# An attention row split anew: seven tiles scaled on ScalarE, outputs scaled with their maximum on VectorE

## The reference, cut to what matters

```python
attn = jnp.einsum('bhnd,bhmd->bhnm', q, k) * attn_scale
attn, a_scale = fq_act(attn)
x_int = x / sf                       # log_int_softmax
x_int = x_int - x_int.max(axis=-1, keepdims=True)
exp_int, _ = _int_exp(x_int, sf)
exp_sum = exp_int.sum(axis=-1, keepdims=True)
ratio = exp_sum / exp_int            # rounded, then to the nearest power of two
attn = jnp.where(mask, 0.0, 2.0 ** (-qlog))
out = jnp.einsum('bhnm,bhmd->bhnd', attn, v)
out, _ = fq_act(out)                 # needs max and min of all outputs
```

## Time and profile before

| quantity | value |
|---|---|
| median of three runs | 1063.03 us (1061.05 to 1063.34) |
| the profiled execution | 1064.02 us, span 1062.2 us |
| VectorE busy | 880.3 us, 83% of the span |
| TensorE busy | 740.5 us, 70% |
| ScalarE busy | 711.8 us, 67% |
| GpSimd busy | 170.0 us, 16% |
| mean granted TensorE clock | 0.837 |

### The profile page before, as it was taken

One profiled execution on the slowest core, in us unless ns is written; L12 is line 12 of the kernel. 1 busy time (PEld: TensorE's weight loads), 2 busy tenths in 40 slices (PEclk: granted clock), 3 DMA queues, 4 the chain that ended last, 5 costly groups with the idle time before them and its releaser, 6 DMA issues. The chain is left out here.

```text
span 1062.2 us, 23653 instructions
## 1 busy us (share of the span) xinstructions
PE 740.5 (70%) x6503; PEld 515.3 (49%) x6504; DVE 880.3 (83%) x2386; ACT 711.8 (67%) x1376; POOL 170.0 (16%) x274
## 2 busy tenths in 40 slices
PE   3772396748888367667667666766532895999997
PEld 3552144425555234434334344433322784889896
DVE  5888986888888799999999999999969632666776
ACT  0353464947888699989989889899750563445543
POOL 5841400016554000000000000000007320000000
PEclk9995598978999687887887788788657676999999
DMA  7000000001111111111110111110040003455452
GB/s 250 3 2 0 0 1 1 0 4 39 37 37 35 32 31 24 25 25 23 23 23 23 26 25 25 23 24 19 12 156 12 1 2 110 147 184 196 166 203 87
DMA packets 84369, 54.61 MB, mean 51 GB/s; under 512 B 53832, under 2 KB 83304, under 8 KB 84072
## 3 DMA queue, kind: packets, MB, share of 16 engines
q1 hardware_dynamic: 83304, 53.97, 16.7%
q0 software_dynamic: 1024, 0.13, 0.2%
HBM read 11.77 MB, written 3.76 MB: 15 GB/s over the span
## 5 line engine op out<-in xcount | busy, mean ns | idle before, releaser
L1370 DVE SCALAR_TENSOR_TENSOR expo<-expo,con,pow 128x153 f32<-128x153 f32 x480 | 146.1, 377 | 1.1 <-ACT expo L1279 1.1
L1148 PE MATMUL at_rem<-word,ident_half 128*128 128x459 f16 x160 | 64.4, 402 | 101.1 <-ACT expo L1279 99.6
L1279 ACT ACTIVATE expo<-at_rem,con 128x459 f32<-128x459 f32 x160 | 95.5, 641 | 12.8 <-PE at_rem L1149 11.4
L953 DVE TENSOR_REDUCE rs_ends<-rs_banks 128x770 f32 (+1 forms) x96 | 91.4, 959 | 14.7 <-PE rs_banks L924 13.7
L873 ACT ACTIVATE rs_banks<-rs_banks 128x770 f32<-128x770 f32 x96 | 76.4, 798 | 25.4 <-PE rs_banks L916 24.2
L1408 DVE CUSTOM_DVE_ANT_0 weight_top<-weight_top,line 128x2448 uint16<-128x2448 uint16 x64 | 86.7, 1354 | 7.1 <-ACT line L1271 3.5
L1148 PEld LDWEIGHTS at_rem<-word,ident_half 128*128 128x128 f16 x160 | 15.6, 97 | 151.7 <-ACT expo L1279 145.6
L1236 ACT ACTIVATE word<-at_banks 128x459 uint8<-128x459 f32 x160 | 79.5, 562 | 8.7 <-PE at_banks L779 8.6
L1229 ACT ACTIVATE pT_all<-at_pT 128x768 bf16<-128x768 int16 (+3 forms) x160 | 79.1, 566 | 7.6 <-PE at_pT L1171 5.7
L774 PE MATMUL at_banks<-pick,row_top 128*128 128x459 bf16 x160 | 72.3, 452 | 13.7 <-ACT word L1236 7.4
L1271 ACT ACTIVATE line<-weight_top 128x1224 f32<-128x1224 f32 x64 | 74.1, 1159 | 10.3 <-DVE weight_top L1398 10.2
(11 more groups left out here) (393 smaller groups left out, 2134.7 us busy)
## 6 DMA issues: line engine op xcount, KB each, us to landing
qk<-vt SPq DMA_DIRECT2D x64, 384.0 KB, 3.0
rs_kb<-qk SPq DMA_DIRECT2D x128, 28.7 KB, 1.9
kb<-qk SPq DMA_DIRECT2D x128, 28.7 KB, 1.9
patches<-in_patches SPq DMA_DIRECT2D x4, 768.0 KB
vi<-vt SPq DMA_DIRECT2D x32, 96.0 KB, 2.0
out<-vi SPq DMA_DIRECT2D x32, 96.0 KB, 1.8
pj_w<-in_w SPq DMA_DIRECT2D x1, 2304.0 KB, 8.3
qb<-qk SPq DMA_DIRECT2D x128, 6.0 KB, 1.8
```

What stands on the lines that cost most here:

```text
L953: v.tensor_reduce(ends[:, :, n, 5 * b:5 * b + 5], banks[:, slot(u, b), :, 0:5 * W].rearrange("p i (t n) -> p i t n", n=W), AX, ALU.max).th ...
L1148: pe.matmul(out, identh[:, :], bank(word, b).bitcast(F16), start=True, stop=False)
L1279: act.activation(bank(ex, b), rem[:, (u + b) % 2, 0:3 * N], ACT.Square, scale=2.0 ** 24, bias=c(5)).then_inc(sq_done, 1)
L1370: ins = v.scalar_tensor_tensor(ex[:, t, :], ex[:, t, :], c(7), pw[:, t, :].bitcast(BF16), ALU.add, ALU.mult, accum_out=tot[:, t:t + 1])
```

## The change

- `both_shares` (ScalarE) multiplies tiles 8 to 14, not 12 to 14. VectorE multiplies tiles 0 to 7 only. `line_of` 1 waits for ScalarE's own products alone.
- `collect` (ScalarE) is gone. VectorE reads the outputs from PSUM, scales, stores and takes their maximum in one TENSOR_TENSOR_REDUCE (`extreme(pair, 0)`), before its pass over `pT_all`; the minimum is taken in the other step of a pair, as before.
- `corner` (ScalarE) and its buffer `p_image` are gone. TensorE transposes those columns straight from the weights, with twelve transposes of 32 columns in the place of three of 128. VectorE's product therefore waits for all of `turn` of the sample before.
- VectorE's order within a step is changed: reciprocal ahead of `octave`, product ahead of `pow`. Its stage is written out for all 34 steps; the other engines keep their loop.

```diff
-                            src = high[:, t, 0:NT] if t < RT else pi[:, 4 * (t - RT):4 * (t - RT) + 4, :].rearrange("p j n -> p (j n)")
-                            mm = pe.transpose(pT[:, slot, j * P:(j + 1) * P], src, identb[:, :])
+                            if t < RT:
+                                mm = pe.transpose(pT[:, slot, j * P:(j + 1) * P], high[:, t, 0:NT], identb[:, :])
+                            else:
+                                for q in range(4):
+                                    mm = pe.transpose(pT[32 * q:32 * q + 32, slot, j * P:(j + 1) * P], high[:, 4 * (t - RT) + q, IW:N], identb[:, :])
...
-                    act.activation(pi[:, :, :].bitcast(I16), high[:, 0:H, IW:N].bitcast(I16), ACT.Copy).then_inc(pi_done, 1)
...
-                    for t in range(H, RT):
+                    for t in range(HALF, RT):
                         ins = act.activation(top[:, t, :], ex[:, t, :], ACT.Copy, scale=inv[:, t:t + 1])
...
-                    act.activation(out_f32(m)[:, pair, :], po[:, 0:HT * N], ACT.Copy, scale=P_UNIT).then_inc(out_done, 1)
...
+                    if kk == 0:
+                        v.wait_ge(pv_done, pair * 2 + 2)
+                        v.tensor_tensor_reduce(out, po[:, 0:HT * N], c(2).to_broadcast([P, HT * N]), 1.0, -BIG, ALU.mult, ALU.max, accum_out=at).then_inc(out_done, 1)
...
-                        for h, half in enumerate(halves):
...
-                            v.tensor_tensor(top[:, heads, :], ex[:, heads, :], share, ALU.mult).then_inc(w_done, 1)
+                        heads = halves[0]
+                        share = inv[:, heads].unsqueeze(2).to_broadcast([P, HALF, N])
+                        v.tensor_tensor(top[:, heads, :], ex[:, heads, :], share, ALU.mult).then_inc(w_done, 1)
...
-                steps(v, body)
+                for n in range(B + 2):
+                    body(n // 2, n % 2)
```

More of the change, by code:

```diff
@@ L1041, in attention @@
         ends_done = k.sem("at_ends_done")
-        pi_done, pj_done, tr_done, ev_done, pv_done, out_done = sem(
-            "pi_done", "pj_done", "tr_done", "ev_done", "pv_done", "out_done")
+        pj_done, tr_done, ev_done, pv_done, out_done = sem(
+            "pj_done", "tr_done", "ev_done", "pv_done", "out_done")
         pj_loaded, a_done = k.sem("pj_loaded"), k.sem("at_a_done")
@@ L1266, in line_of @@
                 def line_of(n, h):
-                    act.wait_ge(w_done, n * 2 + h + 1)
-                    if h == 1:
+                    if h == 0:
+                        act.wait_ge(w_done, n + 1)
+                    else:
                         act.wait_ge(a_done, n + 1)
@@ L1274, in squares @@
                     if not first(n, 1):
-                        act.wait_ge(w_done, n * 2 - (1 if which[0] == 0 else 0))
+                        act.wait_ge(w_done, n)
                     for b in which:
@@ L1279, in squares @@
                         act.activation(bank(ex, b), rem[:, (u + b) % 2, 0:3 * N], ACT.Square, scale=2.0 ** 24, bias=c(5)).then_inc(sq_done, 1)
-                def collect(n, pair):
-                    act.wait_ge(pv_done, n + 1)
-                    act.activation(out_f32(m)[:, pair, :], po[:, 0:HT * N], ACT.Copy, scale=P_UNIT).then_inc(out_done, 1)
                 def body(i, kk):
-                    now, mid, last, gone = (batch(i, kk, lag) for lag in range(4))
+                    now, mid, last = (batch(i, kk, lag) for lag in range(3))
                     if now is not None:
                         distances(now[0])
-                    if gone is not None and gone[1] == 1:
-                        collect(gone[0], gone[2])
                     for chunk in chunks_at(i, kk):
@@ L1294, in body @@
                     if last is not None:
-                        corner(last[0])
                         ranks(last[0], last[1])
@@ L1310, in _ @@
                 steps(act, body)
-                collect(B - 1, B // 2 - 1)
             @block.vector
@@ L1347, in extreme @@
                 def extreme(pair, kk):
[L1349 to L1354 removed]
+                    out, at = out_f32(m)[:, pair, :], m["pj_ext"][:, kk, pair:pair + 1]
+                    if kk == 0:
+                        v.wait_ge(pv_done, pair * 2 + 2)
+                        v.tensor_tensor_reduce(out, po[:, 0:HT * N], c(2).to_broadcast([P, HT * N]), 1.0, -BIG, ALU.mult, ALU.max, accum_out=at).then_inc(out_done, 1)
+                    else:
                         v.wait_ge(out_done, pair + 1)
[L1356 removed]
+                        v.tensor_reduce(at, out, AX, ALU.min, negate=True).then_inc(ends_done, 1)
                 def body(i, kk):
@@ L1375, in body @@
                         v.tensor_scalar(tot[:, :], tot[:, :], LOWER, SHARE, ALU.max, ALU.mult).then_inc(tot_done, 1)
+                        v.wait_ge(tot_done, nb + 1)
+                        v.reciprocal(inv[:, :], tot[:, :]).then_inc(inv_done, 1)
                     if yf is not None:
@@ L1382, in body @@
                     if yb is not None:
-                        v.wait_ge(tot_done, nb + 1)
-                        v.reciprocal(inv[:, :], tot[:, :]).then_inc(inv_done, 1)
+                        v.wait_ge(inv_done, nb + 1)
+                        if not first(nb, 1):
+                            v.wait_ge(tr_done, nb * GROUPS)
+                        heads = halves[0]
+                        share = inv[:, heads].unsqueeze(2).to_broadcast([P, HALF, N])
+                        v.tensor_tensor(top[:, heads, :], ex[:, heads, :], share, ALU.mult).then_inc(w_done, 1)
                     if yf is not None:
@@ L1387, in body @@
                         v.tensor_scalar(pw[:, :, :], oct_[:, :, :], -128.0, 128.0 * (2048 + 63), ALU.mult, ALU.add).then_inc(pw_done, 1)
[L1388 to L1391, removed]
-                        for h, half in enumerate(halves):
[L1393 to L1397, removed]
-                            v.tensor_tensor(top[:, heads, :], ex[:, heads, :], share, ALU.mult).then_inc(w_done, 1)
+                    if kk == 0 and pair is not None:
+                        extreme(pair, 0)
                     if yj is not None:
@@ L1404, in body @@
                         for h, half in enumerate(halves):
-                            if h == 1 and pair is not None:
-                                extreme(pair, kk)
+                            if h == 1 and kk == 1 and pair is not None:
+                                extreme(pair, 1)
                             wait_apart(v, y_done, nb * 2 + h + 1, k.passed)
                             v.tensor_tensor(flat(top, half).bitcast(I32), flat(top, half).bitcast(I32), flat(line, half).bitcast(I32), ALU.add).then_inc(i_done, 1)
-                    elif pair is not None:
-                        extreme(pair, kk)
-                steps(v, body)
+                    elif kk == 1 and pair is not None:
+                        extreme(pair, 1)
+                for n in range(B + 2):
+                    body(n // 2, n % 2)
                 for kk in range(2):
                     extreme(B // 2 - 1, kk)
-                v.wait_ge(ends_done, B)
+                v.wait_ge(ends_done, B // 2)
 def out_f32(m):
```

4 lines of the change are left out of this document (1 added, 3 removed).

## The result

The changed kernel takes 1097.96 us (median of five runs, 1096.64 to 1102.57) against 1061.89 us: a ratio of 1.034, 95% interval 1.032 to 1.037. I had forecast 1075, in a range of 1049 to 1087. It is slower, as forecast, but by three times as much as forecast. The profiled execution has a span of 1100.7 us, 38.5 more than before.

The account below looks back on a forecast made before the run. VectorE was taken to bound the kernel, ScalarE after the change: 12.05 + 0.67 x 1.30 = 12.92 us a step, 0.42 more over 29 steps, +12.2 on 1064.0, less 1.0 for the profiled execution: 1075, range 1049 to 1087.

Parts of the forecast that it names:

- What bounds the kernel before: Attention stage: VectorE, 98% busy, sets the pace at 12.49 us a step; ScalarE, 90% busy, is nearly full.
- VectorE's gain: VectorE's need per step in the attention stage falls from 12.49 to 11.8 us, with the maximum taken at 0.65.
- ScalarE's load: ScalarE's four more tiles cost 1.25 us a step; with both copies dropped it needs 12.05 at high clock.
- `corner` buys nothing at low clock: Dropping this 0.42 us ScalarE copy gains nothing at 1.2 GHz, where the last `ranks` wait for TensorE.
- The clock: TensorE's clock falls after its pause before the first square, for 6.8 us; the pause does not get shorter.
- I keep two in three: Two attention steps in three meet a low TensorE clock, as before, adding 0.67 x 1.30 us to the mean step.
- A step that is hit: An attention step that meets the low TensorE clock takes up to 13.35 us on ScalarE, against 12.05 at high clock.
- The sum: The mean step of 12.92 us against 12.50, over 29 steps, gives +12.2 us and a time of 1075.
- Rival 4: Every attention step meets a low clock stretch: 13.35 us a step, +25 us, 1087; chance 0.06.
- rival 1: ScalarE paces the attention stage but TensorE's clock stays high: 12.05 us a step, 1050; chance 0.15.
- Rival 2: VectorE still paces the attention stage because ScalarE's waits for TensorE close: ScalarE under 11.8 us, 1042; chance 0.15.

Follow-up runs that it names:

- e6: Kernel before, with VectorE making its two products ahead of `pow` instead of behind it: 1057.1 us, ratio 0.993 to 0.998.
- e7: Kernel before, with only VectorE's stage written out for all steps: 1057.1 us, ratio 0.993 to 0.996.
- e11: Kernel before, with e6 and e7 together, ScalarE's two copies kept: 1056.2 us, ratio 0.991 to 0.995.
- e4: Changed kernel with only the split undone (ScalarE tiles 12 to 14, VectorE 0 to 7 and 8 to 11): 1051.0 us, ratio 0.987 to 0.993.
- e1: Changed kernel with 28 unused transposes per step in TensorE's pause: 1050.4 us over six of nine runs; the other three took 1085 to 1100.
- e3: Kernel before, with only the split changed (ScalarE tiles 8 to 14, VectorE 0 to 7): 1095.6 us, ratio 1.026 to 1.037.
- e8: Changed kernel with ScalarE on tiles 10 to 14, VectorE on 0 to 9 in one product, pause not filled: 1063.5 us, ratio 0.999 to 1.002.
- e5: Changed kernel with ScalarE on tiles 10 to 14, VectorE on 0 to 9 in one product, TensorE's pause filled: 1050.2 us, ratio 0.986 to 0.993.
- e9: As e5, but VectorE's product in two, tiles 0 to 7, then 8 and 9: 1047.8 us, ratio 0.982 to 0.987.

## Why the prediction was wrong in size

**What bounds the kernel before**: half right. I took VectorE's 98% for the limit of the step. It was the round VectorE, ScalarE, VectorE, 12.49 us, with VectorE's own work in the loop, 12.43, just beneath it; e6, e7 and e11 show it. The forecast lost nothing by that, since ScalarE was to set the pace.

**VectorE's gain**: undersized. With the same tiles its own need is 12.15 (e4), not 12.5, hence about 11.45 with eight tiles, an estimate that e1 bears out (busy for 288.6 of 302 us, 11.5 a step). The maximum costs 629 ns, near the 0.65 chosen (groups by line of the changed kernel, stage):

```profile
L1339 DVE CUSTOM_DVE_ANT_0 qk<-at_out,con 128x459 f32<-128x459 f32 x11 | 6.9, 629 | 0.0
```

None of it counts, being covered as said. By the Trainium skill (VectorE: DVE Perf Modes, the TRN2 errata) the estimate was 0.60; the trace agrees within 0.03.

**ScalarE's load**: right. Seven tiles follow one another at 0.31 us, 2.19 from 543.84 to 546.03. At high clock the step was to be 12.05; e1 shows 12.02. One comparison there proves less than it says: four small tiles for 1.25 us against one product of 0.71 sets ScalarE against VectorE. On ScalarE alone, the 1224 elements of `line_of` 0 take 1.21 us in one instruction (at 546.03), and eight tiles of 153 would take 8 x 0.31 = 2.5.

**`corner` buys nothing at low clock**: right, e3; nor does `collect`.

**The clock**: the step that failed, "I keep two in three". Every step meets a low stretch, 22 of 22 between 430 and 732 us, where it was 16 of 24. The pause grew from 1.96 to 2.94 us to 3.22; I had argued that it would not get shorter, and drew no more from it. Moreover a step of 13.65 us is just the 6.8 low and 6.8 high that the trace shows, so the low stretch comes back to the same place. e3, which has other work, has the same average. That this locks the two together is my reading; e1's two groups of runs fit it, but no run takes the pause and the length apart.

**A step that is hit**: the second term that was too small, 13.35 forecast, 13.65 measured. I had taken TensorE's chain from a step in which the clock rose just before `turn` 2: 1.57 us from there to ScalarE's tiles, in all 5.67 from the first eviction. Now it lies wholly at low clock: 543.84 - 537.75 = 6.09. Of the 0.42 between them the forecast had 0.1, for the narrow transposes. The trace of the kernel before would have told me, since another step of it, four steps further on, has the whole chain at low clock, 577.25 - 571.18 = 6.07:

```profile
571.18 1.44 ACT L1236 ACTIVATE word<-at_banks 128x459 uint8<-128x459 f32 x3
...
577.25 1.05 ACT L1263 ACTIVATE weight_top<-expo,inv_total 128x153 f32<-128x153 f32 x3
```

The sum by these: 12.92 would have been 13.35 with every step hit (+0.43), and 13.65 with the full chain (+0.30); 29 x 0.73 = 21 of the 23 us by which 1098 exceeds 1075. Rival 4 had this mechanism, every step hit, at 1087 and with a chance of 0.06; its step of 13.35 was short by the same 0.30.

**Rivals 1 and 2**: rival 1's condition is e1. Rival 2's is not met: ScalarE's waits for TensorE did not close.

The Trainium skill, Perfetto Trace Analysis (Optimizing Scalar/DVE Operations), says that moving work off a saturated VectorE to ScalarE may make sense. Here it did not as the clock was: with all else of the change in place, three, five and seven tiles on ScalarE take 1051 (e4), 1063 (e8) and 1098 us. With TensorE's pause filled five tiles take 1050 and 1048 (e5, e9), no clear gain over e4.

## What to carry to other kernels

A busy share of 98% does not prove a bound: look for instructions that start just behind the end of the one before them at a fixed distance from another engine's end, and add up the round. When ScalarE and TensorE exchange small pieces, price the exchange at the low clock, and ask of every change whether it lengthens TensorE's longest pause; 28 transposes whose result nobody used were worth 44 to 48 us here. Try each part of a change by itself: the whole lost 36 us, and all of it but the new split (e4) gained 11. Before moving work from a full engine to one at 90%, subtract the waits that cannot close from the 10%.

## What the runs showed of the hardware

The earlier trace rows show one fall of TensorE's granted clock in the kernel before, with pauses of 1.96 to 2.94 us a step; it falls in 16 of 24 steps there. In the changed kernel, with a pause of 3.22 us, it falls in every step, each time 1.7 us after the pause has ended (547.83, 549.5), and stays at 1.2 GHz for 6.8 us.

Twelve transposes of 32 columns cost about as much as three of 128. From `turn` 2's first transpose to its last group (L1171) pass 542.67 - 541.92 = 0.75 us in the changed kernel and 576.12 - 575.34 = 0.78 us in the kernel before, all at low clock:

```profile
575.34 0.52 PE L1165 MATMUL at_pT<-identb,weight_top 128*128 128x128 bf16 x3
575.66 0.52 PE L1165 MATMUL at_pT<-identb,p_image 128*128 128x128 bf16 x3
576.12 0.25 PE L1171 MATMUL at_pT<-identb,weight_top 128*32 128x32 bf16 x12
```

At high clock it is 0.45 us (e1) against 0.44. The 0.1 us that I had allowed for them was not needed.
